# Cross-attention and FFN on one core: running sums and the reciprocal in PSUM, the last block in other buffers, full q and the stores of the result on ScalarE, all engines in a new order

## What is computed

```python
h = layernorm(x)
q, k, v = h @ Wq, ctx @ Wk, ctx @ Wv           # 16 heads of 32
q, k = headnorm(q) * gq + bq, headnorm(k) * gk + bk
att = softmax(q @ k.T / sqrt(32)) @ v
x = x + att @ Wo
s = layernorm(x) @ Win + bin_                   # 64 units
g = sum_over_16(relu(s * W1 + b1) * W2) + b2    # per unit
out = x + g @ Wout + bout
```

## Time and profile before

| | us |
|---|---|
| median of 3 runs | 531.59 |
| lowest, highest | 526.32, 532.4 |
| the profiled execution, its own time | 534.23 |
| its span, first to last instruction | 532.1 |
| mean granted TensorE clock | 0.951 of full speed |

### The profile page before, as it was taken

One profiled execution on the slowest core, in us unless ns is written; L12 is line 12 of the kernel. 1 busy time (PEld: TensorE's weight loads), 2 busy tenths in 40 slices (PEclk: granted clock), 3 DMA queues, 4 the chain that ended last, 5 costly groups with the idle time before them and its releaser, 6 DMA issues.

```text
span 532.1 us, 7537 instructions
## 1 busy us (share of the span) xinstructions
PE 452.4 (85%) x2392; PEld 304.8 (57%) x2392; DVE 405.1 (76%) x742; ACT 300.7 (57%) x539; POOL 218.4 (41%) x191
## 2 busy tenths in 40 slices
PE   5959957999989997998989998999899967975843
PEld 3646633676657754774567565765567535633732
DVE  3787962798689959994799869987996698546365
ACT  3468445737853688337752876259733872485042
POOL 3247612362555146622465246506554514102330
PEclk9998978999989999898999998999999988998896
DMA  8522576158015830387017811582058107801202
GB/s 309 158 77 81 129 152 139 62 117 198 24 38 151 213 78 21 118 184 176 22 63 165 203 28 45 152 193 51 1 156 202 41 0 179 200 22 59 89 11 79
DMA packets 25206, 58.31 MB, mean 110 GB/s; under 512 B 5840, under 2 KB 6352, under 8 KB 22096
## 3 DMA queue, kind: packets, MB, share of 16 engines
q1 hardware_dynamic: 24912, 57.57, 41.6%
q10 hardware_dynamic: 256, 0.26, 0.2%
HBM read 22.17 MB, written 8.39 MB: 57 GB/s over the span
## 4 chain that ended last, share of the span: by engine, by line
PE 52%; DVE 18%; DMA 8%; SPq 8%; ACT 5%; issue 5%; POOL 3%; DVEq 0%; ACTq 0%; POOLq 0%
PE bank L1719 33%; DVE hid L801 6%; DMA q_stack<-qt_hi 5%; PE bank L1725 5%; PE bank L1806 3%; PE bank L1818 3%; PE bank L1784 3%; ACT hid L1329 3%; PE bank L1821 2%; SPq L304 2%; DVE mx L727 2%; DMA q_stack<-mxt 2%; POOL at_lo L478 2%; SPq L264 2%; DVE at_lo L806 2%
## 5 line engine op out<-in xcount | busy, mean ns | idle before, releaser
L1260 ACT ACTIVATE prob<-bank 128x512 f32<-128x512 f32 x128 | 71.2, 597 | 30.6 <-PE bank L1806 20.1
L727 DVE TENSOR_REDUCE mx<-bank 128x4 f32<-128x512 f32 x128 | 81.0, 681 | 2.9 <-PE bank L1784 2.8
L473 POOL TENSOR_TENSOR qt_lo<-u,qt_hi 128x512 fp32r<-128x512 f32 x32 | 43.2, 1351 | 89.0 <-DVE u L719 89.0
L1818 PE MATMUL bank<-prob,v_kv 128*32 128x512 f32 x256 | 65.1, 622 | 3.4 <-ACT prob L1260 3.4
L462 POOL TENSOR_TENSOR squares<-u 128x512 f32<-128x512 f32 x32 | 36.0, 1124 | 70.9 <-DVE ssq L709 53.4
L1821 PE MATMUL bank<-prob,den_sel 128*32 128x512 f32 x256 | 64.4, 623 | 0.0
L1806 PE MATMUL bank<-q_stack,k_stack 97*128 97x512 f32 x128 | 50.3, 449 | 16.3 <-DMA q_stack<-qt_hi 7.9
L478 POOL TENSOR_TENSOR at_lo<-att,at_hi 128x512 fp32r<-128x512 f32 x32 | 40.4, 1291 | 47.6 <-ACT at_hi L1305 47.4
L1719 PE MATMUL bank<-wo_hi,at_hi 128*128 128x512 f32 x128 | 54.4, 425 | 4.6 <-POOL at_lo L478 4.6
L801 DVE SCALAR_TENSOR_TENSOR hid<-hid,w_col 128x512 f32<-128x512 f32 x56 | 53.4, 954 | 5.5 <-ACT hid L1329 1.6
L1719 PE MATMUL bank<-wq_hi,zt_hi 128*128 128x512 f32 x128 | 54.3, 424 | 3.7 <-DVE zt_lo L703 3.6
(11 more groups left out here) (136 smaller groups left out, 983.3 us busy)
## 6 DMA issues: line engine op xcount, KB each, us to landing
q_stack<-qt_hi SPq DMA_DIRECT2D x64, 256.0 KB, 5.1
xin<-in_x_dram SPq DMA_DIRECT2D x32, 256.0 KB, 3.1
q_stack<-qt_lo SPq DMA_DIRECT2D x32, 256.0 KB, 5.0
x<-in_x_dram SPq DMA_DIRECT2D x32, 256.0 KB, 3.2
out_dram<-x SPq DMA_DIRECT2D x32, 256.0 KB, 2.0
att<-in_L_xattn_Wk_dram SPq DMA_DIRECT2D x1, 1024.0 KB, 6.4
x<-in_L_xattn_Wq_dram SPq DMA_DIRECT2D x4, 256.0 KB, 7.4
hid<-in_L_xattn_Wv_dram SPq DMA_DIRECT2D x1, 1024.0 KB, 10.3
```

Of the source, the lines that this page charges most:

```text
L473: pool.tensor_tensor(qt_lo[:, :, cols], u[:, j, :].rearrange("p (i n) -> p i n", i=HC), qt_hi[:, :, cols].bitcast(F32), ALU.subtract).then ...
L727: dve.tensor_reduce(mx[:, j, :].rearrange("p (g i) -> p i g", g=G)[:, 2 * half:2 * half + 2, 2 * r:2 * r + 2], maxs_banks[T][half][j][r][: ...
L1260: act.activation(prob[:, h % PR, :], score_bank[t][h][:, :], ACT.Exp, scale=SCALE).then_inc(exp_done, 1)
L1818: pe.matmul(at_bank[t][c][rows(n), :], v_kv[kv_of(t)][:, n * HD:(n + 1) * HD], prob[:, n % PR, :], start=True, stop=True)
```

## The change

- The running sum of the hidden units is in the PSUM bank of `project_s` (`s_bank`) instead of `hid` slot 0; all four slots of `hid` now rotate. `g_high` and `g_low` read the bank.
- The Newton step of the reciprocal works in place in the denominators' bank (`den_bank`), and `rden_err` is gone.
- `q_full` runs on ScalarE.
- The last block (t = 7) uses other buffers: `u` for `att`, `wq_hi`/`wq_lo` for `at_hi`/`at_lo`, `qt_hi`/`qt_lo` for z2, `xin` for `x1`.
- The stores of the result are issued by ScalarE, between its activations; SP keeps the loads and `stack_q`.
- All five orders and all bank tables are new. The q work runs one block further ahead: iteration t now has `project_q(t + 2, ...)`.

```diff
-                dve.tensor_tensor(rden_err[:, :], den_bank[t][:, :], rden[:, :], ALU.mult).then_inc(rden_step, 1)
+                dve.tensor_tensor(den_bank[t][:, :], den_bank[t][:, :], rden[:, :], ALU.mult).then_inc(rden_step, 1)
...
-                dve.scalar_tensor_tensor(out=rden[:, :], in0=rden_err[:, :], scalar=2.0, in1=rden[:, :],
+                dve.scalar_tensor_tensor(out=den_bank[t][:, :], in0=den_bank[t][:, :], scalar=2.0, in1=rden[:, :],
                                          op0=ALU.subtract, op1=ALU.mult).then_inc(rden_done, 1)
...
-                dve.scalar_tensor_tensor(out=rden_both, in0=rden[:, :], scalar=low_col[:, 0:1], in1=rden_hi.bitcast(F32),
+                dve.scalar_tensor_tensor(out=rden_both(t), in0=den_bank[t][:, :], scalar=low_col[:, 0:1],
+                                         in1=rden_hi(t).bitcast(F32),
                                          op0=ALU.mult, op1=ALU.subtract).then_inc(rden_both_done, 1)
...
-                    dve.tensor_scalar(hid_slot(0), hid_slot(0), w2_col[:, 0:1], b2_col[:, 0:1], ALU.mult,
+                    dve.tensor_scalar(s_bank[T][:, :], hid[:, 0, :], w2_col[:, 0:1], b2_col[:, 0:1], ALU.mult,
...
-                    dve.scalar_tensor_tensor(out=hid_slot(0), in0=hid_slot(hh), scalar=w2_col[:, hh:hh + 1],
-                                             in1=hid_slot(0), op0=ALU.mult, op1=ALU.add).then_inc(hsum_done, 1)
+                    dve.scalar_tensor_tensor(out=s_bank[T][:, :], in0=hid[:, hh % RR, :], scalar=w2_col[:, hh:hh + 1],
+                                             in1=s_bank[T][:, :], op0=ALU.mult, op1=ALU.add).then_inc(hsum_done, 1)
...
-            def q_full(T, j):
-
-                dve.wait_ge(qt_hi_done, T * TB + j + 1)
-                dve.tensor_scalar(u[:, j, :], qt_bank[T][j][:, :], gq_col[:, 0:1], bq_col[:, 0:1], ALU.mult,
-                                  ALU.add).then_inc(qf_done, 1)
...
+            def store(T, j):
+                act.wait_ge(out_done, T * TB + j + 1)
+                act.dma_start(out_t[T, j], x1_of(T)[:, j, :]).then_inc(stored[j], 16)
+
+            def q_full(T, j):
+
+                act.wait_ge(q_turned, T * TB + j + 1)
+                act.activation(u[:, j, :], qt_bank[T][j][:, :], ACT.Identity, bias=bq_col[:, 0:1],
+                               scale=gq_col[:, 0:1]).then_inc(qf_done, 1)
...
             def att_high(T, c):
                 act.wait_ge(att_done, T * C + c + 1)
-                if not first(T):
+                if last(T):
+                    act.wait_ge(q_done, BLOCKS * TB)
+                elif not first(T):
                     act.wait_ge(s_mm_done, T)
                     if c == 0:
                         act.wait_ge(y_done, T * TB)
...
-        s_bank = [banks[n] for n in (3, 3, 3, 3, 3, 7, 0, 7)]
+        s_bank = [banks[n] for n in (0, 0, 0, 0, 0, 2, 0, 2)]
```

More of the change, by code:

```diff
@@ new lines, in iteration @@
+                q_high(t, 0)
+                q_full(t, 0)
+                if t >= 2:
+                    rden_high(t - 2)
+                if t >= 3:
+                    move_rstd(t - 3)
+                q_high(t, 1)
+                if t >= 3:
+                    hidden(t - 3, 0)
+                if t >= 3:
+                    hidden(t - 3, 1)
+                if t >= 3:
+                    hidden(t - 3, 2)
+                z1_high(t + 1, 2)
+                q_full(t, 1)
+                move_u(t + 1, 0)
@@ L1695, in epilogue @@
                 z2_high(7, 3)
+                g_high(6)
                 guess2(7)
@@ new lines, in epilogue @@
+                scores(6, 3)
+                pe.wait_ge(mx_done[1], 59)
+                spread(5, 2)
+                pe.wait_ge(g_done, 5)
+                project_y(4, 0)
+                pe.wait_ge(qf_done, 31)
+                project_y(4, 1)
+                pe.wait_ge(att_done, 22)
+                project_y(4, 2)
+                pe.wait_ge(exp_done, 100)
+                pe.wait_ge(mx_done[1], 60)
+                values(6, 0)
+                pe.wait_ge(qf_done, 32)
+                scores(6, 4)
@@ new lines, in epilogue @@
+                pe.wait_ge(out_done, 17)
+                project_y(4, 3)
+                pe.wait_ge(att_done, 23)
+                scores(6, 5)
+                pe.wait_ge(out_done, 19)
+                spread(5, 3)
+                pe.wait_ge(mx_done[0], 58)
+                pe.wait_ge(exp_done, 101)
+                max_scores(7, 0, 1)
+                values(6, 1)
+                pe.wait_ge(out_done, 20)
+                scores(6, 6)
+                pe.wait_ge(att_done, 24)
+                scores(6, 7)
@@ new lines, in epilogue @@
+                pe.wait_ge(mx_done[0], 63)
+                values(6, 4)
+                values(6, 5)
+                pe.wait_ge(mx_done[1], 64)
+                scores(6, 12)
+                pe.wait_ge(x1_done, 22)
+                scores(6, 13)
+                turn_z2(5, 0)
+                project_o(5, 2, 1)
+                pe.wait_ge(mx_done[0], 64)
+                turn_max(7)
+                pe.wait_ge(exp_done, 110)
+                project_o(5, 3, 0)
+                pe.wait_ge(mxt_done, 8)
```

2216 lines of the change are left out of this document (1137 added, 1079 removed), and 3 rows, old and new, of the table maxs_rows.

## The result

| | before | after |
|---|---|---|
| median, us | 532.0 (526.32 to 532.73, 4 runs) | 486.42 (485.37 to 487.15, 4 runs) |
| the profiled execution, its span | 534.23, 532.1 | 485.37, 483.6 |
| mean granted TensorE clock | 0.951 | 0.968 |

What follows compares the result with a forecast made beforehand. TensorE, busy 452 of 532 us, was the bound, with 79.7 us idle to win besides the clock. Terms -8.5 - 4.6 - 3.3 + 3.0 - 5.0 - 9.5 = -27.9 us took 534.2 to 506.3, scaled 504; range 488 to 522.

Steps and rivals of the forecast that it cites:

- Sums, `g_low`, `rden_split` in PSUM: In the iterations: sums at 752 ns, 3.8 us off each block's 18.2 us chain to `g_low`; -8.5 us of TensorE waits.
- I leave 0.5 us of it in each iteration: TensorE's wait for `g_low` in front of `project_y` nearly closes; 2.5 us of its 11.0 us stay.
- I allow 3 us of new waits over the five iterations: The sum holds its bank through the eight hidden units, one bank less; +3 us, ends 0 and 10.
- Clock: TensorE's granted clock in the iterations returns from 0.97 to 1.00; at most 6.9 us come back, 5 taken.
- I cost it at nothing: `q_full` on ScalarE: 25.5 us leave VectorE, 25.1 us enter ScalarE, whose slack covers them; 0 us.
- I count no gain for it either: Stores issued by ScalarE win nothing on the transfers; only the earlier issue of `stack_q` was counted.
- Prologue: Before the steady blocks: 3.3 us of DMA waits for `stack_q` go, nothing more; ends -6 and +6.
- Tail: Last block's own buffers: 16.2 us less work ahead of the last `values`, 58.2 us from there to the end; -9.5 us.
- C: Rival: all waits of the iterations close, 22.5 us idle and 6.9 of clock come back; 490 us, chance 0.10.
- B: Rival: the sums in PSUM are no quicker, 954 ns as in SBUF; 517 us, chance 0.10.
- D: Rival, slower: ScalarE is held by its stores and the exponentials behind them wait; 546 us, chance 0.08.
- A: Rival: the iterations' waits only change their name, so only tail and prologue gain; 519 us, chance 0.17.

Runs made afterwards that it cites:

- e1: The changed kernel with the running sum of the MLP kept in an SBUF tensor instead of the bank: 515.58 us, 29.9 more than the changed kernel.
- e2: The changed kernel with `q_full` given back to VectorE, at the times at which ScalarE made it: 501.58 us, 15.9 more.
- e7: The kernel before with only `q_full` moved to ScalarE: 531.31 us, ratio to before 0.998.
- e4: The changed kernel with sums and Newton steps of the reciprocal in SBUF, `q_full` on VectorE and stores on SyncE again: 522.38 us, 0.982 of the time before.
- e3: The changed kernel with the stores issued by SyncE again, each ahead of the load that waits for it: 492.32 us, 6.6 more.
- e11: The changed kernel with another order of its last 30 us, other banks for y and block 6's stores on SyncE: 484.8 us.
- e12: The kernel of e11 with 28 unread matmuls between the last `project_y` of block 6 and the first of block 7: 483.07 us.
- e9: The changed kernel run again unchanged, as the base on its chip: 485.69 us.
- e13: The kernel of e12 with 38 unread matmuls in place of 28: 482.88 us.
- e10: The changed kernel with 8 unread matmuls between the last `project_y` of block 6 and the first of block 7: 484.99 us.

## Why the prediction was right or wrong

The time fell outside the range because one part of the change was priced at nothing although it shortened the chain that sets the period, and because about half of the gain outside the steady blocks had no term. By its own terms the prediction gave a steady block 3.7 us, 11.1 in three (6.3 for `g_low`, 2.8 for `stack_q`, 3.8 for the clock, less 1.8 for new waits); the trace shows 5.7 (17.2). Outside these blocks it gave 16.8 us, and the trace shows 31.3.

- **Sums, `g_low`, `rden_split` in PSUM: right, and too small in the chain.** 751 ns in the mean for 752, `g_low` 681 for 680. The chain from `scale_s` became 13.15 us, 5.1 less than 18.2 where I had taken off 3.8. From start to start, the sums and `g_low` of this block account for 4.5 of the 5.1, since they had been stretched more here than in the mean of all blocks. The rest is the mix: the 18 instructions stayed 18, but two `q_full`, `rden_error` and `rden_fix` made way for `rden_split`, `normalise`, a `z1_low` and a `stats1`, which are a little shorter, and a wait of 0.17 us is gone. I had seen the moves and did not carry them into this sum.
- **Sums in the bank against the new order.** e1 puts them at 29.9 us, where the sum had 8.5 and the clock's 5. Part of this is that with sums in SBUF the new order sets more of them beside GpSimd than the old one did (1.04 us in the mean for 0.95).
- **"I leave 0.5 us of it in each iteration": none was left.** That is 1.5 us in three blocks; e1 and e2 show that instead there is about 1 us of slack.
- **"I allow 3 us of new waits over the five iterations": none in the steady blocks, but 5.0 us behind them.** Idle time in three blocks is 1.9 us, nearly all row maxima. What I called the fifth iteration (338 to 396.59) is by the code the first block of `epilogue()`, with other work around it. It had 4.6 us idle at a clock of 1.00, and the like stretch now, 335 to 385, has 5.1 at 0.93: there the waits did change their names.
- **`stack_q`: right in kind.** Its waits are gone; in these three blocks they were 4.3 us, where I had 2.8.
- **Clock: 3.8 us forecast for three blocks, 4.8 measured.** It goes with the idle time: 1.00 with 0.6 us idle per block, 0.97 with 4.2 (e1) and 4.8 (before), though 1.00 still with 2.4 (e2).
- **"I cost it at nothing" (`q_full` on ScalarE): this is the step that failed most.** The cover I named, ScalarE's slack, is real: its exponentials found it idle for 28.6 us in all before them, against 30.6. But I asked only what the work costs where it arrives. Where it left, it was on the chain that sets the period: e2 prices it at 15.9 us. In the old order it is worth nothing (e7). So neither a price from the old trace alone nor a part tried alone would have shown it. The 15.9 us is its price with all else changed, and part of it is shared with the other parts (e4).
- **Stores, "I count no gain for it either": wrong by up to 6.6 us** (e3). My view was that the transfers share the same engines. The gain shows not in the transfers but in SyncE's order: with the store on the same queue, the next one waits until the last has landed and the load behind it is issued. The wait for a result that I quoted, 176.0 us, was the sign.
- **Prologue: -3.3 forecast; idle time up to `scale_s` of block 0 fell from 23.1 to 12.8 us.** e4 with all the old work has 14.2 there, so most of this is the order, with q one block ahead. I had no term for it beyond the one DMA wait.
- **From the fourth `scale_s` to the last `values`: no term of its own; idle time fell from 19.6 to 7.9 us.** What brought it was not taken apart.
- **Tail: 9.5 us forecast, 6.4 by the same reckoning.** I worked out 58.2 us from the last `values` to the end; it is 61.3 (422.3 to 483.6). Before it was 51.5, without the 16.2 us of work that were moved there, so 6.4 us were gained. I had `project_s` of the last block at full clock (3.05 us); it took 4.6, the first eight of its twelve matmuls at half pace. And I had not seen that bank 7 serves two tiles of y in turn, a wait of 4.0 us.
- **VectorE busy near 358 us: it was 367.9.** 9.0 us of the difference are two small operations of the layer norms' Newton steps (L635 and L638, 16 each): 17.4 us where they had 8.4, since 13 of these 32 now stand beside GpSimd and take over 0.3 us, where 4 did before. The prediction priced only the large operations.
- **Rivals.** C, all waits of the iterations close, 490 us at 0.10, was the nearest, 3.6 us above the median; its objection "2.6 us of row maxima" held, to 1.8. B and D fell by the rows of the sum and of the store (0.34 us, and no wait of TensorE behind one). A fell with the idle time of the steady blocks. I gave A and B 0.27 together, and both stood on the side of less gain. The only case on the other side had 0.10, although the waits that I had priced one by one up to the fifth iteration were 21.5 of 79.7 us idle: the lower end of the range was too near. That the steady blocks came so close to C and the whole still only just missed the range is partly luck, for only half of the gain outside them had been priced.

## What to carry to other kernels

The worth of a part is that of the chain it leaves, in the order it will be in: walk every removed instruction through the chain that ends last, not through the busy time of the engine that takes it over. A VectorE operation with both inputs in SBUF beside GpSimd work is better priced toward its longest time than at its mean, since a new order may put more of them beside it (here the mean went from 0.95 to 1.04 us); one input in PSUM takes the neighbour away. And when a change has several parts, expect them to share slack: here two parts worth 10 us each made 45.6 us together with the stores, and `q_full` on ScalarE was worth nothing alone and 15.9 us with the rest in place.

## What the runs showed of the hardware

- Two SBUF inputs beside GpSimd: 0.75 us becomes 1.2 to 1.8 for a sum of 128x512 (e1), and the same holds for tiny ones: the 128x4 product of the Newton steps takes 0.16 us in the median and 1.2 at worst (the changed kernel). One with a single SBUF tensor as input (`TENSOR_SCALAR`) is stretched as well. Three in a row stand on the way of block 6's rstd in the changed kernel, beside `att_low` and `add_bout`, and take 3.35 us where the fourth takes 0.16:

```profile
439.85 0.94 DVE L633 TENSOR_TENSOR ln<-ln 128x4 f32<-128x4 f32 x1 [0.75 <-ACT ln L1229]
440.83 1.20 DVE L635 SCALAR_TENSOR_TENSOR ln<-mv,ln 128x4 f32<-128x4 f32 x1
442.06 1.21 DVE L638 TENSOR_SCALAR ln<-ln 128x4 f32<-128x4 f32 x1
443.30 0.16 DVE L640 TENSOR_TENSOR ln<-ln 128x4 f32<-128x4 f32 x1
```

- A running sum into a bank costs what the undisturbed SBUF sum costs (median 754 and 750 ns), so no surcharge for PSUM shows in this form.
- A store issued by ScalarE holds its sequencer 0.34 us, less than the 0.53 us of the maxima's transfer; at worst it held it 1.39 us.
- TensorE's granted clock at the end follows the wait just before: 0.68 after 9.3 us without work (e11), 0.80 after 2.9 and 2.5 (e12, e9), 0.93 and 1.00 after 0.6 (e13, e10). The 0.93 is the mean of the stretch: all twelve matmuls of e13 start 0.23 us apart.
